# A normalized attention-and-fractal kernel on one core: where p and q meet, and in which order SyncE loads and stores

## The reference

```python
x = x + L0(gn(x), gamma)     # L0: gamma * (v @ softmax(v^T v)) + v, per image, v = gn(x) as pixels x channels
x = x + L1(gn(x), w1, ...)
def L1(x):
    x = (x - xmin) / (xmax - xmin + EPS)                     # per image
    log_m = log(stack([box_sum(x, k) for k in (2, 4, 8, 16)]) + EPS)
    alphas = slope of log_m over log(scale)
    excite = sigmoid(relu(alphas.mean((1, 2)) @ w1 + b1) @ w2 + b2)   # one factor per image and channel
    sim = cosine similarity of log_m and its fitted line
    return sim * sigmoid(batch_norm(alphas)) + (1 - sim) * x * excite
```

## Time and profile before

| | |
|---|---|
| Time, median of 3 runs | 6618.52 us (6600.68 to 6620.09) |
| Profiled execution, its own time | 6632.39 us |
| Its span in the profile | 6630.7 us |
| Busy: PE, DVE, ACT, POOL | 5047.4 (76%), 5429.1 (82%), 4779.8 (72%), 1760.3 (27%) us |
| Granted TensorE clock, mean | 0.909 of full |
| DMA traffic | 1344.72 MB, mean 203 GB/s |

### The profile page before, as it was taken

One profiled execution on the slowest core, in us unless ns is written; L12 is line 12 of the kernel. 1 busy time (PEld: TensorE's weight loads), 2 busy tenths in 40 slices (PEclk: granted clock), 3 DMA queues, 4 the chain that ended last, 5 costly groups with the idle time before them and its releaser, 6 DMA issues.

```text
span 6630.7 us, 108223 instructions
## 1 busy us (share of the span) xinstructions
PE 5047.4 (76%) x35320; PEld 4635.9 (70%) x35320; DVE 5429.1 (82%) x6453; ACT 4779.8 (72%) x5203; POOL 1760.3 (27%) x1201
## 2 busy tenths in 40 slices
PE   6968887688858888588867888588876877466643
PEld 5757776688848888578857888588866777466642
DVE  1349998699968999699987999699997999599961
ACT  0118887588858888488866888488876888588851
POOL 0022222422233222322214222322214222333310
PEclk9989999899979999799989999799988999788865
DMA  3635554577756777477756777477765666455556
GB/s 115 196 123 169 177 176 150 163 241 245 246 166 204 248 248 241 134 250 249 248 181 195 249 251 242 134 240 251 247 196 176 220 222 223 131 187 180 183 184 228
DMA packets 874519, 1344.72 MB, mean 203 GB/s; under 512 B 38704, under 2 KB 694096, under 8 KB 857936
## 3 DMA queue, kind: packets, MB, share of 16 engines
q1 hardware_dynamic: 837456, 1208.16, 53.2%
q0 software_dynamic: 36864, 134.23, 10.7%
HBM read 671.16 MB, written 536.87 MB: 182 GB/s over the span
## 4 chain that ended last, share of the span: by engine, by line
PE 31%; ACT 18%; DMA 17%; issue 16%; DVE 14%; POOL 3%; SPq 1%; DVEq 0%; ACTq 0%; POOLq 0%
PE even L530 12%; DMA xa<-in_x_dram 7%; DMA x1t<-logs 6%; PE h_ps L511 5%; PE g_ps L488 4%; ACT logs L706 3%; PE odd L530 2%; PE even L532 2%; ACT logs L735 2%; DMA hr<-h_scratch 2%; DVE ut L1013 2%; DMA qd<-q_scratch 2%; PE g_ps L489 2%; ACT logs L722 2%; ACT odd L706 2%
## 5 line engine op out<-in xcount | busy, mean ns | idle before, releaser
L530 PE MATMUL even<-band,t 128*128 128x128 f32 x12288 | 1891.2, 286 | 470.5 <-ACT logs L706 313.2
L530 PEld LDWEIGHTS even<-band,t 128*128 128x128 f32 x12288 | 1660.9, 201 | 525.0 <-issue 448.9
L387 POOL TENSOR_TENSOR t<-t 128x1024 f32<-128x1024 f32 (+3 forms) x800 | 1339.6, 1686 | 1157.6 <-DVE logs L997 1114.6
L706 ACT ACTIVATE logs<-even,col 128x1024 f32<-128x1024 f32 x512 | 571.0, 1115 | 945.5 <-PE even L530 944.8
L511 PE MATMUL h_ps<-mix,xt 128*128 128x256 f32 x4096 | 994.2, 386 | 183.3 <-ACT xt L693 182.6
L428 POOL DMA_DIRECT2D x1t<-logs x256 | 226.4, 884 | 2933.4 <-DVE ut L1013 2863.6
L511 PEld LDWEIGHTS h_ps<-mix,xt 128*128 128x128 f32 x4096 | 737.5, 190 | 313.6 <-ACT xt L693 233.3
L488 PE MATMUL g_ps<-xa 128*128 128x257 f32 x2048 | 652.5, 401 | 259.5 <-DMA xa<-in_x_dram 259.4
L532 PE MATMUL even<-band,t 128*128 128x128 f32 x4096 | 791.9, 275 | 0.0
L892 DVE CUSTOM_DVE_ANT_0 h_out<-h_ps,shift,mx 128x512 f32<-128x512 f32 x512 | 382.9, 748 | 361.3 <-PE h_ps L511 356.7
L532 PEld LDWEIGHTS even<-band,t 128*128 128x128 f32 x4096 | 621.9, 192 | 0.0
(11 more groups left out here) (184 smaller groups left out, 10311.4 us busy)
## 6 DMA issues: line engine op xcount, KB each, us to landing
xa<-in_x_dram SPq DMA_DIRECT2D x256, 512.0 KB, 4.6
xb<-in_x_dram SPq DMA_DIRECT2D x256, 512.0 KB, 5.5
h_scratch<-h_out SPq DMA_DIRECT2D x128, 1024.0 KB, 7.0
hr<-h_scratch SPq DMA_DIRECT2D x256, 512.0 KB, 6.4
q_scratch<-ut SPq DMA_DIRECT2D x256, 512.0 KB, 2.7
x1t<-logs POOLq DMA_DIRECT2D x256, 512.0 KB, 5.1
p_scratch<-x1t SPq DMA_DIRECT2D x256, 512.0 KB, 3.1
pd<-p_scratch SPq DMA_DIRECT2D x256, 512.0 KB, 6.0
```

The lines of the kernel that those rows point to most:

```text
L387: ins = g.tensor_tensor(dst[:, hf, d:d + n, :], src[:, hf, d:d + n, :], src[:, hf, e:e + n, :], ALU.add)
L530: ins = t.matmul(o, src[:, hf, at, :], band[:, which, :], start=True, stop=(which < 3))
L706: a.activation(dst, src[:, :], ACT.Ln, bias=col[:, EPSR:EPSR + 1]).then_inc(log_ready[which], 1)
```

## The change

The change has three parts.

1. **Where p and q meet.** `p_plus_q` on DVE goes, and the tile `pd` with it. SP loads q alone into `qd`. ACT computes `scale_q` in place (qd * NE + KD, at the head of its unit). POOL then issues a DMA that reads p from DRAM and adds it to `qd` in SBUF (`add_p`), and `turn_back` on PE waits for its landing.
2. **What p is.** `x1t` and its ACT pass go. ACT's one offset pass writes (h - min) times the norm factor into `ut`; DVE's gated product goes to `logs` slot 3 instead of `ut`, and is q; the DMA on POOL adds `logs` slot 4 to `ut`, and that is p. The constant that is missing comes in as KD, and NE absorbs the factor. The squares, which write slot 3, now wait for the stores of the unit two before.
3. **SP's order.** The loads of a unit (xa, xb, q) are issued a unit earlier, ahead of `store_pq`.

The core of the diff, with what only renames left out:

```diff
@@ block.sync
             def store_pq(unit, n, hf):
                 sp.wait_ge(tail_done, unit + 1)
                 apart()
-                sp.dma_start(q_dram[unit], ut[:, hf, :]).then_inc(pq_stored[hf], 16)
-                sp.wait_ge(x1_summed[hf], 16 * (n + 1))
+                sp.dma_start(q_dram[unit], logs[:, hf, 3, :]).then_inc(pq_stored[hf], 16)
+                sp.wait_ge(p_summed[hf], 16 * (n + 1))
                 apart()
-                sp.dma_start(p_dram[unit], x1t[:, hf, :]).then_inc(pq_stored[hf], 16)
+                sp.dma_start(p_dram[unit], ut[:, hf, :]).then_inc(pq_stored[hf], 16)
...
+            def loads(s, i, k, hf, A, Bs, Ds):
...
                     sp.wait_ge(o_filled, 2 * ud)
                     apart()
-                    sp.dma_start(pd[:, hf, :], p_dram[ud]).then_inc(pq_loaded[hf], 16)
-                    sp.dma_start(qd[:, hf, :], q_dram[ud]).then_inc(pq_loaded[hf], 16)
+                    sp.dma_start(qd[:, hf, :], q_dram[ud]).then_inc(q_loaded[hf], 16)
...
+                if hf == 0:
+                    loads(s, i, k, 1, A, Bs, Ds)
+                elif k == 0:
+                    loads(s, i, 1, 0, A, Bs, Ds)
+                elif not last:
+                    loads(s, i + 1, 0, 0, A, Bs, Ds)
                 if Cs and not began:
                     store_pq(u - 2, nC - 1, hf)
@@ block.gpsimd
+            def add_p(unit, n, hf):
+                pool.wait_ge(q_scaled, unit + 1)
+                apart()
+                g.dma_start(qd[:, hf, :], p_dram[unit], accum_op=ALU.add).then_inc(sum_ready[hf], 16)
-            def sum_x1(unit, hf):
+            def sum_p(unit, hf):
                 pool.wait_ge(tail_done, unit + 1)
                 apart()
-                g.dma_start(x1t[:, hf, :], logs[:, hf, 4, :], accum_op=ALU.add).then_inc(x1_summed[hf], 16)
+                g.dma_start(ut[:, hf, :], logs[:, hf, 4, :], accum_op=ALU.add).then_inc(p_summed[hf], 16)
...
+                            if Cs and not begin and not (last and k == 1 and hf == 1):
+                                half_chunk(i, k, hf)
+                            if Ds:
+                                add_p(u - 32, 16 * (image - 1) + 2 * i + k, hf)
+                            if Cs and not begin:
+                                sum_p(u - 1, 1 - hf)
@@ block.tensor
             def turn_back(unit, n, hf, d):
                 if d == 0:
-                    pe.wait_ge(sum_ready, unit + 1)
+                    pe.wait_ge(sum_ready[hf], 16 * (n + 1))
@@ block.scalar
-                a.activation(ut[:, hf, :], odd[:, :], ACT.Identity, bias=col[:, NEGMIN:NEGMIN + 1]).then_inc(ut_ready, 1)
-                a.activation(x1t[:, hf, :], odd[:, :], ACT.Identity, bias=col[:, XK + hf:XK + hf + 1],
-                             scale=col[:, XS + hf:XS + hf + 1]).then_inc(x1_ready, 1)
+                a.activation(ut[:, hf, :], odd[:, :], ACT.Identity, bias=col[:, XK + hf:XK + hf + 1],
+                             scale=col[:, XS + hf:XS + hf + 1]).then_inc(ut_ready, 1)
+            def scale_q(unit, n, hf):
+                act.wait_ge(q_loaded[hf], 16 * (n + 1))
+                a.activation(qd[:, hf, :], qd[:, hf, :], ACT.Identity, bias=col[:, KD + hf:KD + hf + 1],
+                             scale=col[:, NE + hf:NE + hf + 1]).then_inc(q_scaled, 1)
@@ block.vector
-            def p_plus_q(n, unit, hf):
-                dve.wait_ge(pq_loaded[hf], 32 * (n + 1))
-                d.scalar_tensor_tensor(pd[:, hf, :], qd[:, hf, :], cols(NE)[:, hf:hf + 1], pd[:, hf, :],
-                                       ALU.mult, ALU.add).then_inc(sum_ready, 1)
```

More of the change, by code:

```diff
@@ L268, in half_chunk @@
                 if Ds:
[L269 to L272, removed]
                     sp.wait_ge(o_filled, 2 * ud)
                     apart()
-                    sp.dma_start(pd[:, hf, :], p_dram[ud]).then_inc(pq_loaded[hf], 16)
-                    sp.dma_start(qd[:, hf, :], q_dram[ud]).then_inc(pq_loaded[hf], 16)
+                    sp.dma_start(qd[:, hf, :], q_dram[ud]).then_inc(q_loaded[hf], 16)
+            def half_chunk(s, i, k, hf, A, Bs, Cs, Ds, first, last):
+                n = 16 * s + 2 * i + k
+                nb, nC, nd = n - 16, n - 32, n - 48
+                u = 2 * nC + hf
+                began = first and k == 0
                 if Cs and not (began and hf == 0) and not (last and (k, hf) != (0, 0)):
@@ L308, in turn @@
                             load_rows(first + m, 1 - m, hf)
+                if Ds:
+                    for p in pq_stored:
+                        sp.wait_ge(p, 32 * CHUNKS * (s - 2))
+                        apart()
+                loads(s, 0, 0, 0, A, Bs, Ds)
                 def pair(i, first, last):
@@ L444, in turn, with half_chunk, pair @@
                             more_row_sums(1 - m, hf, 34 * image + 2 * m + hf + 1)
[L446 to L463, removed]
+                def half_chunk(i, k, hf):
+                    u = 32 * image + 4 * i + 2 * k + hf
+                    pool.wait_ge(z_ready, u)
+                    more_row_sums(1 - k if hf == 1 else k, 1 - hf, u + 4 + 2 * image)
+                def pair(i, first, last):
+                    for k in range(2):
+                        for hf in range(2):
+                            u = 32 * image + 4 * i + 2 * k + hf
+                            begin = first and k == 0 and hf == 0
+                            if Cs and not begin and not (last and k == 1 and hf == 1):
+                                half_chunk(i, k, hf)
+                            if Ds:
+                                add_p(u - 32, 16 * (image - 1) + 2 * i + k, hf)
+                            if Cs and not begin:
+                                sum_p(u - 1, 1 - hf)
+                pair(0, True, False)
+                with own.loop(1, PAIRS - 1, POOL_PAIR if Cs else 0) as i:
+                    pair(i, False, False)
+                pair(PAIRS - 1, False, True)
                 if Bs:
@@ L706, in log, with offset @@
                 a.activation(dst, src[:, :], ACT.Ln, bias=col[:, EPSR:EPSR + 1]).then_inc(log_ready[which], 1)
[L708 removed]
+            def offset(unit, n, hf):
                 act.wait_ge(odd_filled, 2 * unit + 2)
@@ L767, in half_chunk @@
                 tail = Cs and not first
+                if Ds:
+                    scale_q(ud, nd, hf)
                 if tail:
-                    offset_and_x1(u - 1, nC if hf == 1 else nC - 1, 1 - hf)
+                    offset(u - 1, nC if hf == 1 else nC - 1, 1 - hf)
                 if Cs:
@@ L1130, in value_range @@
                 d.tensor_copy(cols(XS), cols(RI)).then_inc(dve_done, own.one())
-                d.tensor_copy(cols(XK), cols(M1)).then_inc(dve_done, own.one())
+                d.tensor_scalar(cols(XK), cols(RI), col[:, NEGMIN:NEGMIN + 1], None, ALU.mult).then_inc(dve_done, own.one())
+                dve.wait_ge(dve_done, own.now())
+                d.tensor_tensor(late[:, KX], cols(M1), cols(XK), ALU.subtract).then_inc(dve_done, own.one())
+                d.tensor_scalar(late[:, IV], cols(R1), col[:, INV:INV + 1], None, ALU.mult).then_inc(dve_done, own.one())
                 dve.wait_ge(dve_done, own.now())
```

74 lines of the change are left out of this document (41 added, 33 removed).

## The result

| | before | after |
|---|---|---|
| Time, median of 4 runs | 6619.31 us (6600.68 to 6631.02) | 9068.35 us (9057.65 to 9074.62) |
| Ratio, 95% interval | | 1.370 (1.367 to 1.374) |
| Span of the profiled execution | 6630.7 us | 9065.5 us |
| Mean granted TensorE clock | 0.909 | 0.794 |

What follows compares the result with a forecast made beforehand. DVE was taken as nearly full, a chain of waits through SyncE's queue costing it 4%. 6632 - 30 (loads) + 2383 (turns 3 to 9) + 136 (turn 10) = 9121, less 14 for the median: about 9110 us, range 8600 to 9750.

Steps and rivals of the forecast that it cites:

- Turn 10: Output-only turn: each unit becomes serial, 10.9 us instead of 6.66, over 32 units +136 us, bounds +100 to +185.
- The loop: Turns 3 to 9: norm, row sums, add, turn_back and next norm form a closed cycle, 32.45 us per unit instead of 21.17.
- norm to the DMA's issue: On POOL: row sums start 0.21 us after the norm, work 5.17, and the add is issued 0.57 later.
- transfer to turn_back: The accumulating DMA of p from DRAM, until turn_back can start: 5.5 us, bounds 4.5 and 7.0.
- turn_back to DVE's copy: On PE: turn_back and gram matmuls 3.6 us, mix_x 2.0, then 0.2 to DVE; 5.8 us.
- copy to the end of the next norm: On DVE: 16.94 us before, less 1.2 for p_plus_q and 0.5 of idle time; 15.2 us.
- The slow restart: PE, idle for 12 us, restarts at low clock, doubling the first 1.9 us to 3.6; 1.7 us per unit.
- Rival B: The add lands before PE comes to turn_back, so the kernel gets faster, about 6300 us; chance 5%.
- Rival C: Other work overlaps part of the add's wait: +3 to +7 us per unit, 7400 to 8200 us; chance 8%.
- Rival D: PE's clock stays low through turn_h, gram and boxes: up to +7 us per unit more, 10600 us; chance 7%.
- E: The loads issued earlier gain nothing in turn 2, 9140 us; counted inside the forecast, with no chance of its own.
- The term of 30 us: Gain in turn 2 from earlier loads, with DVE's busy time as next bound; taken from 0 to 54 us.

Runs made afterwards that it cites:

- e4: The changed kernel with the accumulating DMA adding only the first half of p's columns, 256 KB; 8699 us, ratio 1.315.
- e9: The changed kernel with 12 matmuls of zeros on PE ahead of its wait for the add in turns 3 to 9; 8747 us, ratio 1.322.
- e5: The changed kernel with the add of unit u+1 issued on POOL behind unit u's row sums, ahead of the DMA making p of u-1; 6752 us, ratio 1.020.
- e10: The changed kernel with SyncE's loads again behind the stores of q and p, as before the change; 9455 us, ratio 1.429.
- e7: e5, and in turn 10 ACT scales q of the next unit ahead of this unit's output copies; 6667 us, ratio 1.007.
- e2: The changed kernel with the add issued on POOL ahead of its own unit's row sums; 7963 us, ratio 1.204.
- e1: The kernel before with only SP's new order, a unit's loads ahead of the stores of q and p; 6557 us, ratio 0.990.
- e8: The changed kernel with 22 matmuls of zeros on PE ahead of its wait for the add in turns 3 to 9; 10479 us, ratio 1.583.

## Why the prediction was right, step by step

The forecast was 9110 us, and 9068 came. By the segments: turns 0 to 2 were to give 30 us and gave 44. Turns 3 to 9 were to cost 2383 and cost 2293. Turn 10 was to cost 136 and cost 186. The sum is +2489 against +2435 in the spans. The mechanism was right; that the total is off by 0.5% only is in part luck, since the misses of -90 and +50 us in the two costs offset each other.

**The loop.** Each term of the 32.45 us has its row in the unit above:

| term | forecast | measured in this unit | mean of the full turns |
|---|---|---|---|
| norm to the DMA's issue | 5.95 | 6164.80 - 6159.81 = 4.99 | 5.2 |
| transfer to turn_back | 5.5 | 6170.26 - 6164.80 = 5.46 | 5.6 |
| turn_back to DVE's copy | 5.8 | 6175.90 - 6170.26 = 5.64 | 6.1 |
| copy to the end of the next norm | 15.2 | 6190.85 - 6175.90 = 14.95 | 15.15 |
| sum | 32.45 | 31.04 | 32.0 |

(The means are over the fourth to the thirtieth unit of turns 3 to 7, from norm to norm; the 31.74 above have a unit of 26 us near the turn's end in them.) The one that was mis-sized is the first: I had taken 0.57 us for the issue from a DMA that was waiting in the queue, but here POOL goes from its last row sum to the DMA without a gap. The transfer from DRAM was near the one from SBUF (5.4 against 5.1 us), as I had taken it, and e4 shows that nearly all of it is on the loop. The slow restart was forecast at 1.7 us, and e9 shows 2.0 in a full turn.

**The turns.** Per unit of a full turn the loss was 31.74 - 21.1 = 10.6 us, where 11.3 were forecast. A full turn lost (5492 - 3792) / 5 = 340 us, where 349 were forecast. With 30 units at 10.6 that leaves 22 us for the first and the last unit and the turn's ends, where I had 10, with 22 as the bound: two misses that offset each other. Turns 8 and 9 were forecast at 638 us and cost 593.

**The mechanism** was argued from the queues alone, and e5 shows it: with the add in another place of POOL's queue the loss in turns 3 to 9 is gone. Rival B (it lands in time) needed an issue that early, and the changed kernel doesn't have it. Rival C (the link partly hidden, +3 to +7 us per unit) falls with the unit's 10.6. Rival D (the clock stays low through the unit) falls with the profile: the granted clock is 0.52 from turn_back to mix_x and 1.00 behind it, where turn_h, the gram and the boxes are still to come. E (the moved loads do nothing) falls with turns 0 to 2: 1142 us, and 1182 in e10, where only the loads are late again.

**Loads.** That DVE's busy time is the bound in turn 2 held, though its size was misread: from 583.51 to 1105.78 us there are 26 starts of L1013, so 25 units and not 26, and the old pace is 20.9 us, not 20.09. Its starts before, then in turn 2 of the changed kernel, and the latter's window:

```profile
L1013 DVE SCALAR_TENSOR_TENSOR ut<-logs,ut x26: 1208/1218/1226, 583.5 to 1105.8; 128x1024 f32<-128x1024 f32 x26
```

```profile
L1044 DVE SCALAR_TENSOR_TENSOR logs<-logs,ut x29: 1208/1216/1226, 562.3 to 1101.4; 128x1024 f32<-128x1024 f32 x29
500.00:1120.00 620.00, 533.15 (x3946) 497.47 (x3945) 601.25 (x701) 523.47 (x534) 174.20 (x120) 0.98 0.57 179
```

With 20.9 the bound is 564.37 / 620 x 20.9 = 19.0 us, and not 18.3. The unit now takes (1101.4 - 562.3) / 28 = 19.25 us, with DVE busy 97%. The term of 30 us took about half of the possible gain, and 44 came. The squares' new wait for the stores, costed at nothing, isn't among the waits of ACT and DVE in the changed kernel.

**Turn 10** is the step that was too cheap. I had 10.9 us per unit with a transfer of 5.5. Timelines of POOL, PE and SP in turn 10:

```profile
8902.24 0.86 POOL L443 DMA_DIRECT2D qd<-p_scratch  x1 [13.11 <-ACT qd L743]
...
8907.87 1.11 PE L571 MATMUL o_ps<-ident,qd 128*128 128x128 f32 x4 [8.09 <-DMA qd<-p_scratch]
...
8911.65 0.41 SPq L295 DMA_DIRECT2D out_dram<-o_sb  x1
8912.41 13.29 SPq L272 DMA_DIRECT2D qd<-q_scratch  x2
8913.26 0.86 POOL L443 DMA_DIRECT2D qd<-p_scratch  x1 [10.16 <-ACT qd L743]
...
8922.13 1.11 PE L571 MATMUL o_ps<-ident,qd 128*128 128x128 f32 x4 [11.35 <-DMA qd<-p_scratch]
...
8933.13 1.11 PE L571 MATMUL o_ps<-ident,qd 128*128 128x128 f32 x4 [8.00 <-DMA qd<-p_scratch]
```

Every second add goes out beside the 1 MB store of the output and a load of q, and takes 8.9 us to turn_back where the other takes 5.6. Two units take 8933.13 - 8907.87 = 25.3 us, 12.6 each; the surplus over 10.9 is 1.7 x 32 = 54 us, about the miss of 50. I had put the price of the transfer at the quiet value, although the bound of 7.0 us stood beside it. That the store and the load beside it make it late fits e7, where the adds of turn 10 are issued at another moment and all but one land in 5.6 us or less.

## What to carry to other kernels

A DMA is an instruction of the queue that issues it: before moving work to an engine that is idle 73% of the time, list what stands ahead of it there, what each of those waits for, and whether that closes a loop with the one who waits for the DMA. Moving it "first" helps only if it is also not behind the last wait of the round before (e2 against e5). And when a link is cut, read the busy share of the next engine first: what that engine has left, and not the length of the wait, bounds what the cut can bring (e1).

## What the runs showed of the hardware

- The same accumulating DMA of 512 KB took from issue to landing 5.4 (changed kernel), 7.4 (e10), 7.9 (e2) or 8.8 us (e5), all medians, by the place at which it or the loads were issued. The landing time doesn't tell what it costs: with 5.4 us PE waited 2765 us for it, with 8.8 us 358.
- From issue to landing, 256 KB took 3.9 us and 512 KB 5.4 (e4).
- A filler of zeros during a wait of 11 us kept PE's restart at full speed, and the kernel got 3.5% faster by doing 12 useless matmuls per unit (e9). A float32 matmul of 128x512 took 0.86 us at a granted clock of 1.00 (22 in 18.9 us, e8), and has two records in the trace (x44 for 22).
